# Weight quantisation, K and V preparation merged into the attention of a transformer block on one core

## The reference

```python
def block(x, ctx):                       # x: (4, 2048, 512) f32, ctx: (4, 77, 512) f32
    x = x + xattn(layernorm(x), ctx, ctx, Wq, Wo)       # 16 heads of 32
    x = x + ffn(layernorm(x), clip_x, clip_down, w_gate, w_up, w_down)
    return x
# xattn: Q, K, V = q @ Wq.T, k @ Wq.T, v @ Wq.T; softmax(Q K^T / sqrt(32)) V, then @ Wo.T
# fake_quant(a, clip): scale = sigmoid(clip) * max|a| / 127 over the whole tensor; round(a / scale) * scale
# weight_quant(w): scale = max|row| / 127 for each row
# ffn: xq = fake_quant(x, clip_x); h = silu(xq @ wq(w_gate).T) * (xq @ wq(w_up).T)    # inner 1408
#      fake_quant(h, clip_down) @ wq(w_down).T
```

## Time and profile before

| | |
|---|---|
| median of three runs | 1257.39 us |
| the profiled execution | 1256.07 us |
| its span, first to last instruction | 1253.9 us |
| TensorE matmul busy | 1148.4 us, 92% |
| VectorE busy | 871.8 us, 70% |
| ScalarE busy | 683.7 us, 55% |
| GpSimd busy | 120.9 us, 10% |
| granted TensorE clock, mean | 0.964 |

### The profile page before, as it was taken

The page is one execution under the profiler, slowest core; times in us unless marked ns, Lnnn a source line. Parts: engine busy times, 40 slices in busy tenths (PEclk is TensorE's granted clock), DMA queues, the critical chain, the costliest instruction groups (busy, mean ns, idle before and its releaser), DMA issues. The chain is left out here.

```text
span 1253.9 us, 17607 instructions
## 1 busy us (share of the span) xinstructions
PE 1148.4 (92%) x6508; PEld 651.9 (52%) x6508; DVE 871.8 (70%) x1559; ACT 683.7 (55%) x829; POOL 120.9 (10%) x80
## 2 busy tenths in 40 slices
PE   6457899999999999999999955999999999699898
PEld 4345566666666666666666432444444444244333
DVE  5866577777777777777766553777777777575475
ACT  5744655555555555655554514656666665744440
POOL 0100000000000000000000000000000000165677
PEclk9769999999999999999999977999999999799999
DMA  9841122223222232221112256766777722599977
GB/s 355 323 155 43 51 68 77 91 87 112 76 76 77 81 115 83 86 76 60 51 51 66 70 177 208 250 228 231 243 228 239 246 69 84 232 405 421 418 278 262
DMA packets 112188, 205.37 MB, mean 164 GB/s; under 512 B 40711, under 2 KB 47623, under 8 KB 106095
## 3 DMA queue, kind: packets, MB, share of 16 engines
q1 hardware_dynamic: 112111, 204.34, 46.6%
HBM read 119.02 MB, written 76.90 MB: 156 GB/s over the span
## 5 line engine op out<-in xcount | busy, mean ns | idle before, releaser
L947 PE MATMUL e_G<-e_cT,e_gu 128*128 128x512 bf16 x704 | 182.4, 382 | 27.3 <-DMA e_cT<-e_cb 27.3
L655 PE MATMUL a_Q<-a_xnT,wq 128*128 128x512 f32 x768 | 195.9, 404 | 8.7 <-DVE a_xnT L640 7.7
L920 DVE SCALAR_TENSOR_TENSOR h<-e_U,x_gus,e_sg 128x512 f32<-128x512 f32 x176 | 131.9, 750 | 84.9 <-PE e_U L951 59.1
L869 ACT ACTIVATE e_sg<-e_G,x_gus 128x512 f32<-128x512 f32 x176 | 119.2, 686 | 124.2 <-PE e_G L947 124.2
L655 PEld LDWEIGHTS a_Q<-a_xnT,wq 128*128 128x128 f32 x768 | 140.8, 190 | 86.8 <-issue 58.0
L699 PE MATMUL a_O<-a_wo,a_aT 128*128 128x512 f32 x720 | 183.6, 403 | 0.0
L951 PE MATMUL e_U<-e_cT,e_gu 128*128 128x512 bf16 x704 | 181.7, 381 | 0.0
L1083 PE MATMUL c_Y<-dn,c_cb 128*128 128x512 bf16 x704 | 159.0, 389 | 18.7 <-DVE c_cb L1046 18.7
L699 PEld LDWEIGHTS a_O<-a_wo,a_aT 128*128 128x128 f32 x720 | 130.5, 188 | 46.5 <-issue 19.2
L556 ACT ACTIVATE a_pr<-a_S 77x2048 f32<-77x2048 f32 x64 | 120.2, 1878 | 26.4 <-PE a_S L677 26.4
L947 PEld LDWEIGHTS e_G<-e_cT,e_gu 128*128 128x128 bf16 x704 | 69.1, 98 | 111.5 <-DMA e_cT<-e_cb 27.7
(11 more groups left out here) (135 smaller groups left out, 1306.8 us busy)
## 6 DMA issues: line engine op xcount, KB each, us to landing
x<-x_d SPq DMA_DIRECT2D x32, 1024.0 KB, 7.8
h_d<-h SPq DMA_DIRECT2D x24, 1024.0 KB, 4.1
h<-h_d SPq DMA_DIRECT2D x11, 1536.0 KB, 18.7
a_xr<-in_x SPq DMA_DIRECT2D x64, 256.0 KB, 2.7
x_d<-a_xr SPq DMA_DIRECT2D x64, 256.0 KB, 2.0
out<-c_y SPq DMA_DIRECT2D x15, 1024.0 KB, 11.3
xa<-in_x SPq DMA_DIRECT2D x56, 256.0 KB, 2.7
h<-h_d SPq DMA_DIRECT2D x11, 1280.0 KB, 15.0
```

The costliest lines, as they stand in the source:

```text
L655: mm = nc.tensor.matmul(Q[:], wq[:, wp, j, P * n.g:P * (n.g + 1)], xnT[:, n.par, xp, j], start=(ins == 0), stop=(ins == 3 * KT - 1))
L869: nc.scalar.activation(sg[:, s], G[:, t % GU], ACT.Silu, scale=gus[:, t:t + 1]).then_inc(silued, 1)
L920: nc.vector.scalar_tensor_tensor(out=h[:, place(u, p), t], in0=U[:, t % GU], scalar=gus[:, IT + t:IT + t + 1], in1=sg[:, s], op0=ALU.mult, ...
L947: mm = nc.tensor.matmul(G[:, t % GU], gu[:, k, P * t:P * (t + 1)], cT[:, p, k], start=(k == 0), stop=(k == KT - 1))
```

## The change

- `prepare` is gone. `attend` loads WqT, ctxT and x itself; K is computed ahead of the slots, V of batch b in slot b-5; K and V of all four batches stay in SBUF. `kbd` is built on GpSimd (`spread_k`), and so are the low parts of ctxT and WoT.
- The weights pass through the slots in 46 steps from slot 1 on, one a slot: SP loads a piece of up to 128x512, a slot later VectorE takes its row maxima and makes the scale (`measure`), ACT codes it and GpSimd casts it; then SP turns it with a transposing DMA, and a slot later stores it. The down rows have three pieces, each loaded twice: three steps measure, three code.
- The slot's order and lags change: S of item k-2 comes first, then Q of k+4, the turn of the maxima (now at k % 4 == 1), m_scored of k+3, O of k-7, the turn of tile k+8, DN and then A of k-2. ACT takes the exponential of S ahead of aT; VectorE takes `att`, statistics and moments ahead of the maximum over the scores. The ring of x has six tiles, loaded one slot ahead of their statistics; `rcp` shares `lnd`'s memory. There is one slot more.
- gu, the first two blocks of x1 and dn are loaded in slots 60 to 65 of the attention, into memory that wq, xnT and x had. The wait for the stores of x1 moves from the attention's end to the loads that read them and to VectorE's first write of h.
- Both maxima over partitions: VectorE copies the column to 128, TensorE transposes it, VectorE reduces.
- gu and dn are laid out in turned 128x128 squares; the cast buffer of the contraction lies in gu's memory.

```diff
...
-RINGQ = 6
...
+RINGQ = 7
+RINGX = 6
...
+W_FIRST = 1
...
-            return Q if k >= 6 else O if k >= 0 else (O, A, DN)[k % 3]
+            return Q if k >= 7 else O if k >= -4 else (O, A, DN, Q)[k % 4]
...
+                def store_weight(w):
+                    sp.wait_ge(w_turned[w.ring], 16 * (w.code // 2 + 1))
+                    dst = dn_d[w.row, :, D * w.c:D * w.c + w.width] if w.down else gu_d[w.i]
+                    sp.dma_start(dst, wT[:, w.ring, 0:w.width // P].rearrange("p k n -> p (k n)")).then_inc(w_out[w.ring], 16)
...
-                    if (n := at(k, -4)):
+                    if (n := at(k, -5)):
                         if n.n < 4:
                             sp.wait_ge(w_split, 2)
                         after(sp, x1_out[n.g], 16 * n.block, 1 << 30)
+                        after(sp, mom_rdy, n.n - 3)
                         sp.dma_start(xr[:, n.g], x_t[n.block, n.g]).then_inc(xr_in[n.g], 16)
-                    if (n := at(k, -7)):
-                        sp.wait_ge(mom_rdy, n.n + 1)
+                    if (n := at(k, -8)):
+                        sp.wait_ge(x1_rdy, n.n + 1)
                         sp.dma_start(x1_d[n.block, n.g], xr[:, n.g]).then_inc(x1_out[n.g], 16)
-                    if (n := at(k, 16)) and n.n >= 8:
-                        after(sp, transposed, n.n - 7)
-                        sp.dma_start(xa[:, n.par, n.g], x_t[n.block, n.g]).then_inc(xa_in[n.par][n.g], 16)
...
+                    if (n := at(k, 13)) and n.n >= RINGX:
+                        sp.wait_ge(transposed, n.n - RINGX + 1)
+                        sp.dma_start(xa[:, n.n % RINGX], x_t[n.block, n.g]).then_inc(xa_in[n.n % RINGX], 16)
+                    if (w := weight(k - W_FIRST - 3)) and w.coded:
+                        store_weight(w)
+                    if (w := weight(k - W_FIRST - 2)) and w.coded:
+                        turn_weight(w)
+                    if (w := weight(k - W_FIRST)):
+                        load_weight(w)
...
+                    if 0 <= c < len(GU_CHUNKS):
+                        sp.wait_ge(q_done, STEPS)
+                        a, z = GU_CHUNKS[c]
+                        for h in range(2):
+                            sp.dma_start(gu[:, IT * h + a:IT * h + z].rearrange("p t k n -> p t (k n)"),
+                                         gu_d[IT * h + a:IT * h + z].rearrange("t p n -> p t n")).then_inc(gu_in[c], 16)
+                    if 3 <= c < 5:
+                        for g in range(TT):
+                            sp.wait_ge(x1_out[g], 16 * (c - 2))
+                        sp.dma_start(x1[:, c - 3], x1_d[c - 3].rearrange("t p d -> p t d")).then_inc(x1_in[c - 3], 16)
+                    if c == 5:
+                        sp.wait_ge(transposed, STEPS)
+                        sp.dma_start(dn[:].rearrange("p r k n -> p r (k n)"), dn_d.rearrange("r p n -> p r n")).then_inc(dn_in, 16)
...
+                for k in SLOTS:
+                    if (w := weight(k - W_FIRST - 1)) and w.coded:
+                        pool.wait_ge(w_coded, w.code + 1)
+                        after(pool, w_turned[w.ring], 16 * (w.code // 2), 1 << 30)
+                        nc.gpsimd.tensor_copy(wb[:, w.ring, 0:w.width], wc[:, w.ring, 0:w.width]).then_inc(w_cast, 1)
...
+                    done = at(k, -3)
                     if done:
-                        act.wait_ge(valued, done.n + 1)
+                        act.wait_ge(summed, done.n + 1)
+                        after(act, att_rdy, done.n)
                         nc.scalar.activation(lnd[:], DN[:], ACT.Ln).then_inc(ln_done, 1)
                         act.wait_ge(ln_done, done.n + 1)
-                        after(act, att_rdy, done.n)
                         nc.scalar.activation(rcp[:], lnd[:], ACT.Exp, scale=-1.0).then_inc(rcp_rdy, 1)
...
+                    now = at(k, -2)
+                    if now:
+                        act.wait_ge(scored, now.n + 1)
+                        after(act, valued, now.n)
+                        nc.scalar.activation(pr[:], S[0:KEYS], ACT.Exp, scale=SM_SCALE).then_inc(exped, 1)
...
+                    if (w := weight(k - W_FIRST - 1)) and w.coded:
+                        act.wait_ge(w_raw_in[w.raw], 16 * (w.i // 2 + 1))
+                        act.wait_ge(w_scaled, w.scale + 1)
+                        after(act, w_cast, w.code - 1)
+                        nc.scalar.activation(wc[:, w.ring, 0:w.width], wraw[:, w.raw, 0:w.width], ACT.Copy,
+                                             scale=winv[:, w.scale:w.scale + 1]).then_inc(w_coded, 1)
...
+                def measure(w):
+                    dve.wait_ge(w_raw_in[w.raw], 16 * (w.i // 2 + 1))
+                    col = slice(w.scale, w.scale + 1)
+                    top = dmax[:, w.c:w.c + 1] if w.down else wmax[:, col]
+                    nc.vector.tensor_reduce(top, wraw[:, w.raw, 0:w.width], AX.X, ALU.max, apply_absolute_value=True).then_inc(w_measured, 1)
+                    if w.last:
+                        dve.wait_ge(w_measured, 2 * IT + DCH * w.row + w.c + 1 if w.down else w.i + 1)
+                        if w.down:
+                            own.step(nc.vector.tensor_reduce(wmax[:, col], dmax[:], AX.X, ALU.max))
+                        sc = dsc[:, w.row:w.row + 1] if w.down else wscale[:, col]
+                        own.step(nc.vector.tensor_scalar(sc, wmax[:, col], 1.0 / QMAX, None, ALU.mult))
+                        nc.vector.reciprocal(winv[:, col], sc).then_inc(w_scaled, 1)
...
+                    if done:
+                        dve.wait_ge(aT_h, done.n + 1)
+                        after(dve, projected, TT * (done.block - 1))
+                        nc.vector.tensor_tensor(aT[:, done.par, 1, done.g], att[:], aT[:, done.par, 0, done.g].bitcast(F32),
+                                                ALU.subtract).then_inc(aT_l, 1)
+                    if (w := weight(k - W_FIRST - 1)) and w.measured:
+                        measure(w)
+                    if k % 4 == 1 and (n := at(k, -1)):
+                        dve.wait_ge(m_turned, n.block + 1)
+                        nc.vector.tensor_copy(mT[:], A[:]).then_inc(mT_rdy, 1)
...
+                    if b == 0:
+                        pe.wait_ge(xnT_l, 3)
+                    after(pe, v_rdy, b - 1)
...
+                    now = at(k, -2)
+                    if now:
...
+                    if k % 4 == 1 and (n := at(k, -1)):
...
+                    if (n := at(k, 3)):
+                        after(pe, exped, n.n - 4)
+                        after(pe, maxed, n.n)
...
+                        pe.wait_ge(qT_h, n.n + 1)
+                        for t in range(TT):
+                            mm = nc.tensor.matmul(S[:, t, 0:HG * KEYS], qT[:, n.ring, 0, P * t:P * (t + 1)],
+                                                  kbd[:, n.batch % 2, n.g].rearrange("p h k -> p (h k)"), start=True, stop=True)
+                        mm.then_inc(m_scored, 1)
+                    if (n := at(k, -7)):
...
+                    if 0 <= k + 5 < BATCH:
+                        project_v(k + 5)
...
+                            mm = nc.tensor.matmul(DN[DH * h:DH * (h + 1)], ones[:], pr[:, h], start=True, stop=True)
+                        mm.then_inc(summed, 1)
                         for h in range(HG):
-                            mm = nc.tensor.matmul(DN[DH * h:DH * (h + 1)], ones[:], pr[:, h], start=True, stop=True)
+                            mm = nc.tensor.matmul(A[DH * h:DH * (h + 1)], v[:, now.batch, P * now.g + DH * h:P * now.g + DH * (h + 1)],
+                                                  pr[:, h], start=True, stop=True)
                         mm.then_inc(valued, 1)
...
```

The seams and the FFN:

```diff
...
-                nc.vector.tensor_reduce(tmax[:], hi[:], AX.X, ALU.max).then_inc(s_tmax, 1)
+                own.step(nc.vector.tensor_reduce(tmax[:], hi[:], AX.X, ALU.max))
+                nc.vector.tensor_copy(tall[:], tmax[:].to_broadcast([P, P])).then_inc(s_tmax, 1)
                 dve.wait_ge(s_gmax, 1)
+                own.step(nc.vector.tensor_reduce(gmax[:], M[:, 0:P], AX.X, ALU.max))
...
+                for g in range(TT):
+                    dve.wait_ge(x1_out[g], 16 * BLOCKS)
...
+                pe.wait_ge(s_tmax, 1)
+                nc.tensor.transpose(M[:, 0:P], tall[:], id32[:]).then_inc(s_gmax, 1)
...
-        cb = sb("c_cb", [P, 2, IT, TOK], BF16)
+        cb = gu[:].rearrange("p t k n -> p (t k n)").rearrange("p (b t n) -> p b t n", b=2, t=IT)
...
```

More of the change, by code:

```diff
@@ L402, in __init__, with attend @@
         self.par, self.batch, self.ring = self.block % 2, self.block // BPB, n % RINGQ
-RINGQ = 6
-def attend(nc, x_t, WoT, negsel, kbd_d, kst_d, v_d, x1_d, id32, mom, wq, xa):
+RINGQ = 7
+RINGX = 6
+class Step:
+    def __init__(self, i):
+        self.i, self.raw = i, i % 2
+        self.down = i >= 2 * IT
+        self.row, c = divmod(i - 2 * IT, 2 * DCH) if self.down else (i, 0)
+        self.measured = not self.down or c < DCH
```

(48 more changed lines are left out.)

606 lines of the change are left out of this document (223 added, 383 removed).

## The result

| | us | against before |
|---|---|---|
| before, four runs beside the changed kernel | 1257.48 (1254.40 to 1261.95) | |
| changed, four runs | 1200.77 (1199.83 to 1202.63) | ratio 0.955, 95% interval 0.952 to 0.958 |
| forecast | 1213 (1194 to 1240) | |

What follows compares the result with a forecast made beforehand. TensorE was taken to bound the attention's steady slots. Start -36.1, slots -1.4, drain +1.9, first seam -7.8 and second +0.6 gave -42.8 on the 1253.9 us span: 1211.1, or 1213 executed; range 1194 to 1240.

Steps and rivals of the forecast that it cites:

- Start: Preparation moved into the attention: Q(0) at 26.3, first S at 71.7 instead of 107.8, saving 36.1 us.
- Slots: Attention from the first S: 58 slots in 580 us against 59 in 581.4 before, -1.4 us.
- the same VectorE loop: Attention slots: the turn waits for qT's low part behind VectorE's piece measurement and maximum, 10.2 us a slot, early ones included.
- The steady slot: Attention: the new TensorE order gives 9.6 us without a weight piece, 10.2 with a measured one.
- rival D: Attention slots without a piece stay at 9.9, as Q's 0.3 does not go: 1220 us, chance 0.08.
- Drain: Attention's end, slots without Q: 52.9 us against 51.0 before, +1.9.
- five slots save 3.2: Attention's end: slots without Q fall from 6.46 to 5.8 us, as the exponential now comes first on ACT.
- First seam: Attention to FFN: 24.7 becomes 16.9 us; moved store wait -2.1, maximum -5.7, early loads 0.
- Second seam: The FFN's second maximum over partitions, now by copy, transpose and reduction: costs +0.6 us (0 to +1.5).
- A: Attention: VectorE's loop does not bind and all slots run at 9.6: 1197 us, chance 0.17.
- B: Attention: piece slots 0.5 us dearer through ACT's code, prologue 6 longer: 1236 us, chance 0.23.
- C: Piece traffic on SP and GpSimd holds the attention; decides from 0.95 us on each piece slot, slower than before, chance 0.06.

Runs made afterwards that it cites:

- the edit that puts the tile first: Changed kernel with ACT normalising the next tile of x ahead of copying Q's high part, up to slot 6: 1190.5 us.
- the edit with O ahead: Changed kernel with O issued before m_scored from slot 60 on: 1196.1 us.
- the reduction twice: Changed kernel with the VectorE reduction that measures each weight piece done two times: 1220.3 us.
- both seam edits: Changed kernel with gu, x1 and dn loaded at the expansion's start again and the first seam's maximum back on GpSimd: 1204.0 us.

## Why the prediction came out as it did

**Start (-36.1, measured -33.3).** The mechanism held: one V piece before Q and three in the fill, Q(0) at 28.44 where 26.3 was worked out, and 46.1 us from Q(0) to the first S against 45.4. The 2.1 us before Q(0) are in K. The forecast put it at 8 to 18, while the row that it names has it from 11.08 to 20.6 before the change; here it ran from 7.59 to 20.1, with 1.55 us of waiting for WqT's low part (L490), so that the first tile was turned at 19.95 and not at 18. In the fill the forecast's chain had ACT's order (Q, its copy, the next tile, its turn) and priced it by the slots of before; each such turn waits 0.5 to 1.5 us for the normalised tile, and the edit that puts the tile first takes 1.1 off a fill slot. Half-clock stretches and VectorE's maximum were given 1.6 us together; Q(4) and Q(5) took 5.46 and 4.59 in place of 2.9, which is 4.2 us for the clock alone.

**Slots (-1.4, measured -18.8): here a step failed.** It is the sentence "The early slots ... gain nothing from its absence any more, since they lie under the same VectorE loop". They do not. The loop closes through the bank: the turn waits for qT's low part only where both use bank Q, and that begins at slot 7. In slots 2 to 6 the turn writes O. The five took 40.2 us where the forecast's arithmetic had about 51.9. These 11.7 us are as much as the whole error of 12.0; the others cancel (piece slots 5.7 and the FFN stages 2.5 too long in the forecast, start 2.8 and drain 5.1 too short), and that they do is luck. The experiment with the bank shows it: with the turn in Q's bank from slot 2 they take 61.2. That O is missing there, the rival of that experiment, is not enough: without the bank's loop they are short, with it they are long, and O is missing in both. The kernel before chooses the bank in the same way, from slot 6, in the code quoted ahead of the prediction; the forecast used it for the steady slot and not for these.

The steady slot was right in its mechanism. Slots without a piece were forecast at 9.6 and took 9.65 where they had taken 9.90, so the new order paid 0.25 of its 0.3, and rival D falls. The turn between DN and A, which brings back two changes, costs 0.28 for the two; by that price one is worth about 0.14, and whether the rest of the 0.25 is in other gaps of the new order, or a change behind Q costs more than one behind a turn, is open. From Q's weights to those of m_scored are 2.63 us (226.87 to 229.50), where Q to S, weights and matmuls alike, took 2.97: behind Q, 0.34 went. The rule of the Trainium skill that the prediction weighed (TensorEngine Tiling (Array Packing), Key Properties: changing the mode drains the engine) agrees with that in sign; it gives no price. Slots with a piece were mis-sized: 10.2 forecast, 9.93 measured. TensorE came to the turn as late as 7.0 after S (225.78 to 232.78), but qT's low part was done at 7.5, not 7.6, and the turn, DN and A took 2.44 to the next S (233.28 to 235.72), not 2.6. Slots 7 to 23 and the four with the last piece of a down row are 21, and some 0.27 in each makes 5.7.

**Drain (+1.9, measured +7.0).** The slot without Q was right (5.8 forecast, 5.9 measured). The transition to it was not seen: m_scored stands behind the exponential, in slots up to 59 under Q's 2.6 us and in slot 60 under nothing. The stall is 1.99 us, O then runs at half clock for 1.6 us more, and the edit with O ahead takes back 3.6. The forecast had "five slots save 3.2" and took all of them for alike.

**First seam (-7.8, measured -7.8).** The sum is right, by luck; its parts were credited wrongly. The forecast gave 5.7 to the maximum, 2.1 to the moved wait and 0 to the early loads. In the changed kernel the loads are worth 4.6 of the seam (21.7 against 17.1), the reduction 2.1 with early loads and 0.4 with late ones; both together 5.0, and the moved wait 2.2, the idle time of VectorE ahead of the seam's first instruction (2.53 before, 0.33 after). That leaves 0.5 of the whole 7.7 (24.8 against 17.1) without a place. The reduction at its price of before, 7.07 us from x_tmax to the next step (744.96 to 752.03), came to 3.89 in the changed surroundings and the new way to 1.38 (697.67 to 699.05). The reading that the loads did not hold coding back in the kernel before was true: it waited for the scale. But the next step is the transposing DMA, and the first of those landed at 763.0, 0.4 us behind the load of dn: the loads ran under the slow reduction, and a shorter one alone would have run into them, as the 0.4 above says.

**Second seam, expansion, contraction.** +0.6, as forecast (copy to 128, transpose, reduction: 1.2 us from h_tmax to h_sh). The other two came out 2.5 shorter together, against a forecast of 0; why is open.

**Rivals.** A (all slots at 9.6) is refuted by 9.93 and the waits of 10.5 us, although the time is within 4 us of its 1197: it is the early slots that bring the total there, so that it comes so close is luck. B and C saw the pieces' coding and their traffic on SP and GpSimd hold the slots: VectorE's passes keep their times (the maximum 1.43 us on average before and 1.44 after), GpSimd casts a piece in 0.61, and no wait of TensorE's is put down to a DMA in the slots. B's other part, a start 6 us longer than forecast, was 2.8. C's point of decision, 0.95 us on each piece slot above 10.2, was never near.

## What to carry to other kernels

When a slot is bounded by an order of instructions, ask for which slots the edge that closes the loop exists: here a choice of bank, in one line, took the loop away from five of 58 slots, and that error was as large as the total's. Then look at the first slot in which a stage falls away, because whatever lay hidden under that stage appears there. And price parts of a seam together: two that run beside each other are worth less one by one (from the slow seam of 22.1 us, 0.4 for the reduction and 2.9 for the loads) than together (5.0).

## What the runs showed of the hardware

- TensorE's clock after a pause is not the same from one execution to the next. Slot 60's pause is 1.99 us in each; O behind it took 4.51 us in the changed kernel, at a mean granted clock of 0.62 (part of the stretch at 1.2 GHz), and 2.90 in three of the edited ones. In the same way Q(4), behind a pause of 2.40 us, took 5.46 in some profiled executions and 4.56 to 4.58 in others, and Q(5) 4.58 or 3.00. Together they put the first S at 74.5 (the changed kernel) or at 72.0 (the experiments with the reduction twice and with both seam edits, which touch nothing ahead of it). A difference of 2.5 us in one profiled start says nothing; that is why the totals here go by medians.
- VectorE waited 6.85 us for the first reduction over partitions on GpSimd in the kernel before and 4.92 in the changed one, both with loads running, and 3.67 without loads, after GpSimd had been idle for 681, 179 and 180 us. The loads' share is 1.25 of it, by the two runs of the changed kernel; why the kernel before took 1.9 more stays open. The Trainium skill (GPSIMD Engine Reference, the software stack's dispatch step) gives about 6 us for a first call; two of these three are below.
- A transposing DMA issued behind loads on the same queues landed only when they had: the first turned tile 0.4 to 0.6 us after the last load in three kernels, up to 9.2 us after its issue, and 2.4 us after its issue with no load ahead.
- What GpSimd's casts cost VectorE beside them these runs do not show: in the steady slots the cast starts as VectorE's pass over the turned tile ends (225.31 against 224.67 + 0.69), and the passes around it stay at 0.68 to 0.69 us.
